# Cross attention: one copy for inputs and context, one for queries and keys, and the biases as one-row products on TensorE

## The reference

```
q = (query @ Wq.T + bq)   k = (key @ Wk.T + bk)   v = (value @ Wv.T + bv)     # query: layernorm(x); key, value: the context
scores = einsum('bhtd,bhsd->bhts', q, k) * D ** -0.5 + attn_mask              # D = 8
scores = where(pad, -inf, scores) + spatial_bias + directional_bias           # both are the same tensor (32, 16, 128, 128)
x = x + (softmax(scores) @ v) @ Wo.T + bo
```

## Time and profile before

| | |
|---|---|
| time, three runs | 644.36, 644.40, 647.64 us; median 644.4 |
| profiled execution | 645.74 us, span of its records 644.0 us |
| mean granted TensorE clock | 0.938 of full speed |
| busy over the span | PE 530.0, PEld 412.1, DVE 492.7, ACT 431.3, POOL 384.1 us |

### The profile page before, as it was taken

The page is one execution under the profiler, slowest core; times in us unless marked ns, Lnnn a source line. Parts: engine busy times, 40 slices in busy tenths (PEclk is TensorE's granted clock), DMA queues, the critical chain, the costliest instruction groups (busy, mean ns, idle before and its releaser), DMA issues.

```text
span 644.0 us, 16022 instructions
## 1 busy us (share of the span) xinstructions
PE 530.0 (82%) x4272; PEld 412.1 (64%) x4272; DVE 492.7 (77%) x1988; ACT 431.3 (67%) x1553; POOL 384.1 (60%) x430
## 2 busy tenths in 40 slices
PE   3589999999998967787777778777767699999986
PEld 2367877877877845555555555555545588788864
DVE  0446768777776646899999999999986788888872
ACT  3655687677776336899999999999995133333321
POOL 5124585564667467688888888888860444444430
PEclk9778999999999776998999998999996599999999
DMA  5930000000000334677777778888810000000000
GB/s 131 210 61 1 2 1 1 0 0 0 0 2 1 70 70 83 117 140 145 143 140 138 139 145 150 144 146 148 146 19 1 0 18 16 18 16 16 18 18 16
DMA packets 87512, 42.38 MB, mean 66 GB/s; under 512 B 7467, under 2 KB 87221, under 8 KB 87477
## 3 DMA queue, kind: packets, MB, share of 16 engines
q1 hardware_dynamic: 87476, 41.97, 34.7%
HBM read 39.86 MB, written 2.10 MB: 65 GB/s over the span
## 4 chain that ended last, share of the span: by engine, by line
PE 37%; DVE 17%; issue 8%; ACT 4%; DVEq 1%; POOL 1%; ACTq 0%; POOLq 0%
PE banks L1246 10%; DVE c_P L1037 8%; PE banks L932 5%; PE banks L1270 5%; PE banks L888 3%; ACT c_P L976 2%; PE banks L943 2%; DVE shared L1066 1%; DVE c_min L1037 1%; PE banks L468 1%; ACT shared L1303 1%; PE banks L919 1%; PE banks L898 1%; PE banks L1233 1%; PE banks L1240 1%
## 5 line engine op out<-in xcount | busy, mean ns | idle before, releaser
L976 ACT ACTIVATE c_P<-c_P,c_min 128x128 f32<-128x128 f32 x512 | 201.3, 425 | 0.0
L873 POOL TENSOR_TENSOR c_bias<-c_fside,c_cm 128x2048 f32<-128x2048 f32 x32 | 145.5, 4546 | 3.4 <-DVE c_cm L867 3.4
L1037 DVE CUSTOM_DVE_ANT_0 c_P<-banks,c_bias 128x128 f32<-128x128 f32 x512 | 117.1, 286 | 12.6 <-PE banks L888 7.4
L976 ACT ACTIVATION_READ_ACCUMULATOR c_P<-c_P,c_min 128x1 f32 x512 | 114.8, 224 | 0.0
L932 PE MATMUL banks<-ident,c_P 128*128 128x128 f32 x512 | 83.6, 294 | 5.5 <-ACT c_P L976 3.5
L932 PEld LDWEIGHTS banks<-ident,c_P 128*128 128x128 f32 x512 | 61.2, 150 | 18.7 <-ACT c_P L976 11.1
L1066 DVE COPY shared<-banks 128x512 f32<-128x512 f32 x96 | 65.9, 687 | 6.0 <-PE banks L932 6.0
L1481 POOL TENSOR_TENSOR xs<-shared,xs 128x512 fp32r<-128x512 f32 x8 | 10.8, 1352 | 87.0 <-ACT xs L1313 87.0
L1246 PE MATMUL banks<-um,lb_s 128*128 128x512 f32 x192 | 56.1, 407 | 2.7 <-ACT shared L1303 1.9
L919 PE MATMUL banks<-x_wT,shared 128*128 128x128 f32 x64 | 15.5, 326 | 40.2 <-DVE shared L1061 40.2
L1303 ACT ACTIVATE shared<-banks,bi_col 128x512 f32<-128x512 f32 x32 | 22.0, 688 | 39.2 <-PE banks L1246 39.2
(11 more groups left out here) (196 smaller groups left out, 1407.9 us busy)
## 6 DMA issues: line engine op xcount, KB each, us to landing
c_fside<-in_fside_Bx16xSxS_dram SPq DMA_DIRECT2D x64, 512.0 KB, 7.2
X<-in_x_dram SPq DMA_DIRECT2D x4, 512.0 KB, 5.0
c_ctx<-in_ctx_dram SPq DMA_DIRECT2D x32, 64.0 KB, 5.2
out_dram<-shared SPq DMA_DIRECT2D x8, 256.0 KB, 2.3
kmask_sb<-in_mask_BxS_bf_dram SPq DMA_DIRECT2D x1, 512.0 KB, 7.2
c_P<-in_L_ffn_wi_dram SPq DMA_DIRECT2D x1, 256.0 KB
c_P<-in_L_ffn_wo_dram SPq DMA_DIRECT2D x1, 256.0 KB
c_P<-in_L_ffn_lora_B_dram SPq DMA_DIRECT2D x4, 64.0 KB
```

The lines of the kernel that those rows point to most:

```text
L873: nc.gpsimd.tensor_tensor(fm[:, q, :, :], fs[:, q, :, :], bc(cm[:], XH), ALU.add).then_inc(C["fm"], 1)
L976: last = nc.scalar.activation(P[:, par, h, :], P[:, par, h, :], ACT.Exp, bias=mn[:, par, h:h + 1], scale=-1.0, accum_out=rsx[:, par, h:h + 1])
L1037: last = nc.vector.tensor_tensor_reduce(out=P[:, o, h, :], in0=score_bank(n + 1, i)[:, 128 * j:128 * j + 128], in1=fm[:, o, h, :], scale=- ...
```

## The change

The normalised input and the context are copied out of bank 0 by one instruction of 256 columns into a common tile, and so are queries and keys, by a plain copy. Their biases are put into the bank by TensorE: ahead of each projection a product of the bias row (one partition, 128 columns) with a row of ones. The scale of the queries moves into the weights and the bias row at setup. The block-diagonal keys are built from the new tile, which is double, so the wait of ScalarE for GpSimd loosens by one batch.

```diff
-        bq_raw = sb("bq_raw", [128, 1])
-        bq_col = sb("bq_col", [128, 1])
-        bk_col = sb("bk_col", [128, 1])
+        bias_rows = sb("bias_rows", [1, 3, 128])
+        bq_row, bk_row, bo_row = (bias_rows[:, i, :] for i in range(3))
...
-            for dst, src in ((bq_raw, x_bq), (bk_col, x_bk), (bv_col, x_bv)):
-                sp.dma_start(dst[:], src[:, None]).then_inc(s_xw, 16)
-            sp.dma_start(bo_row[:], x_bo[None, :]).then_inc(s_xw, 16)
+            for dst, src in ((bq_row, x_bq), (bk_row, x_bk), (bo_row, x_bo)):
+                sp.dma_start(dst, src[None, :]).then_inc(s_xw, 16)
+            sp.dma_start(bv_col[:], x_bv[:, None]).then_inc(s_xw, 16)
...
-            nc.scalar.copy(x_wT[:].rearrange("p i d -> p (i d)"), bank(6)).then_inc(s_wcopy, 1)
+            nc.scalar.activation(x_wT[:, 0, :], bank(6)[:, 0:128], ACT.Copy, scale=0.5 * float(XD) ** -0.5)
+            nc.scalar.copy(x_wT[:, 1:4, :].rearrange("p i d -> p (i d)"), bank(6)[:, 128:512]).then_inc(s_wcopy, 1)
...
-            nc.vector.tensor_scalar(bq_col[:], bq_raw[:], 0.5 * float(XD) ** -0.5, None, ALU.mult)
+            nc.vector.tensor_scalar(bq_row, bq_row, 0.5 * float(XD) ** -0.5, None, ALU.mult)
...
             def queries_keys():
                 need(pe, C["T"], n + 3)
-                nc.tensor.matmul(bank(0)[:, 0:128], x_wT[:, 0, :], xT2[:], start=True, stop=True)
-                nc.tensor.matmul(bank(0)[:, 128:256], x_wT[:, 1, :], cT[:, q, :], start=True, stop=True).then_inc(C["qkp"], 1)
+                for w, row in ((0, bq_row), (1, bk_row)):
+                    place = bank(0)[:, 128 * w:128 * w + 128]
+                    nc.tensor.matmul(place, row, ones[0:1, :], start=True, stop=False)
+                    last = nc.tensor.matmul(place, x_wT[:, w, :], xcT[:, q, w, :], start=False, stop=True)
+                last.then_inc(C["qkp"], 1)
...
-                nc.scalar.copy(xT2[:], bank(0)[:, 0:128])
-                nc.scalar.copy(cT[:, q, :], bank(0)[:, 128:256]).then_inc(C["T"], 1)
+                nc.scalar.copy(xcT[:, q, :, :].rearrange("p w t -> p (w t)"), bank(0)[:, 0:256]).then_inc(C["T"], 1)
...
-                nc.scalar.activation(qx[:, q, :], bank(0)[:, 0:128], ACT.Identity, bias=bq_col[:],
-                                     scale=0.5 * float(XD) ** -0.5).then_inc(C["q"], 1)
-                need(act, C["kbd"], n + 2)
-                nc.scalar.activation(kx[:], bank(0)[:, 128:256], ACT.Identity, bias=bk_col[:]).then_inc(C["k"], 1)
+                need(act, C["kbd"], n + 1)
+                nc.scalar.copy(qk[:, q, :, :].rearrange("p w t -> p (w t)"), bank(0)[:, 0:256]).then_inc(C["qk"], 1)
...
-                need(pool, C["k"], n + 3)
+                need(pool, C["qk"], n + 3)
                 need(pool, C["sc"], 4 * n + 4)
-                nc.gpsimd.tensor_tensor(kbd[:, q, :, :], bc(kx[:], XG), inner(k_mask[:], 128), ALU.mult).then_inc(C["kbd"], 1)
+                nc.gpsimd.tensor_tensor(kbd[:, q, :, :], bc(qk[:, q, 1, :], XG), inner(k_mask[:], 128), ALU.mult).then_inc(C["kbd"], 1)
```

More of the change, by code:

```diff
@@ L91, in decoder @@
         x_wT = sb("x_wT", [128, 4, 128])
-        bq_raw = sb("bq_raw", [128, 1])
-        bq_col = sb("bq_col", [128, 1])
-        bk_col = sb("bk_col", [128, 1])
+        bias_rows = sb("bias_rows", [1, 3, 128])
+        bq_row, bk_row, bo_row = (bias_rows[:, i, :] for i in range(3))
         bv_col = sb("bv_col", [128, 1])
         bv_wide = sb("bv_wide", [128, 128])
-        bo_row = sb("bo_row", [1, 128])
         x_bias = sb("x_bias", [128, 128])
@@ L132, in decoder @@
         lb_s = sb("lb_s", [128, 2, F], fp32r)
-        SHARED = 20736
+        SHARED = 18432
         shared = sb("shared", [128, SHARED])
@@ L279, in setup_tensor_2 @@
             nc.tensor.matmul(bank(6)[:, 0:128], bv_wide[:], x_wT[:, 3, :], start=True, stop=False)
-            nc.tensor.matmul(bank(6)[:, 0:128], ones[0:1, :], bo_row[:], start=False, stop=True)
+            nc.tensor.matmul(bank(6)[:, 0:128], ones[0:1, :], bo_row, start=False, stop=True)
             for c in range(FC):
@@ L827, in decoder @@
         xn2 = sb("c_xn", [128, 128])
-        cT = sb("c_cT", [128, 2, 128])
-        qx = sb("c_q", [128, 2, 128])
-        kx = sb("c_k", [128, 128])
+        xcT = sb("c_xcT", [128, 2, 2, 128])
+        qk = sb("c_qk", [128, 2, 2, 128])
         VPAD = XG * (32 + XD)
@@ L839, in decoder @@
         PTs = carve([128, 2, NI, 512])
-        xT2 = carve([128, 128])
         rx = carve([128, XH, XD])
@@ L845, in decoder @@
         C = {n: sem("c_" + n) for n in (
-            "stats", "aggr", "vareps", "rstd", "xn", "xbias", "Tp", "T", "qkp", "q", "k", "kbd", "cm", "fm",
+            "stats", "aggr", "vareps", "rstd", "xn", "xbias", "Tp", "T", "qkp", "qk", "kbd", "cm", "fm",
             "sc", "tt", "ex", "rc", "rx", "Rp", "RT", "pt", "ptD", "ptA", "pv", "oT", "yv", "v", "x2")}
@@ L879, in all_scores @@
             def all_scores():
-                need(pe, C["q"], n + 2)
+                need(pe, C["qk"], n + 2)
                 need(pe, C["kbd"], n + 2)
@@ L887, in all_scores @@
                     rows = slice(32 * i, 32 * i + 32)
-                    nc.tensor.matmul(score_bank(n + 1, i), qx[rows, o, :], kbd[rows, o, :, :].rearrange("p j s -> p (j s)"),
+                    nc.tensor.matmul(score_bank(n + 1, i), qk[rows, o, 0, :], kbd[rows, o, :, :].rearrange("p j s -> p (j s)"),
                                      start=True, stop=True).then_inc(C["sc"], 1)
@@ L907, in queries_keys @@
                 need(pe, C["T"], n + 3)
-                nc.tensor.matmul(bank(0)[:, 0:128], x_wT[:, 0, :], xT2[:], start=True, stop=True)
-                nc.tensor.matmul(bank(0)[:, 128:256], x_wT[:, 1, :], cT[:, q, :], start=True, stop=True).then_inc(C["qkp"], 1)
+                for w, row in ((0, bq_row), (1, bk_row)):
[3 more added lines that the diff above has]
+                last.then_inc(C["qkp"], 1)
             def outputs_values():
                 if project:
-                    need(pe, C["k"], n + 3)
+                    need(pe, C["qk"], n + 3)
                 else:
@@ L920, in outputs_values @@
                 if scores:
-                    last = nc.tensor.matmul(bank(0)[:, 128:256], cT[:, o, :], x_wT[:, 2, :], start=True, stop=True)
+                    last = nc.tensor.matmul(bank(0)[:, 128:256], xcT[:, o, 1, :], x_wT[:, 2, :], start=True, stop=True)
                 last.then_inc(C["yv"], 1)
```

## The result

The changed kernel takes 668.65 us, the median of four executions (662.75 to 669.18), where the kernel before takes 644.76 us beside it (644.36 to 647.64). The estimated ratio is 1.032, with a 95% interval of 1.028 to 1.037 (the two medians alone give 1.037). It is slower, as forecast, but by 24 us where 7.8 were forecast, and 12.7 us beyond the end of the range. The profiled execution has a span of 667.5 us against 644.0. Three of the four executions lie at 668.1 to 669.2 us with a mean granted clock of 0.922, the profiled one among them; the fourth took 662.75 us at 0.934.

The account below looks back on a forecast made before the run. VectorE was taken as the bound, with ScalarE a near miss. Steady stage 3.8, transition 3.8 and setup 0.2 made + 7.8 us on the median 644.4: 652.2 us, range 644.5 to 656 us.

Parts of the forecast that it names:

- near miss: Steady stage: ScalarE, though 100% busy, needs 7.62 us a batch against VectorE's 7.675, so it is not the bound.
- second rival: Steady stage: ScalarE is the bound after all, 7.6 us come off, 638 us in all; chance 0.13.
- The two instructions that ScalarE saves: Cross attention: merged copies and plain copies without bias save ScalarE 0.27 us a batch.
- the ring: Steady stage: ScalarE and TensorE wait on each other in a loop of 7.88 us, exceeding VectorE's 7.675; chance 0.48.
- 0.16 us a switch: TensorE's projections: cost of each change between one row and 128 at 2.4 GHz; four, with passes, make 1.08 us a batch.
- first rival: Added one-row products cost their passes alone, 0.44 us, within the margin of 0.59; 646.3 us in all; chance 0.27.
- the middle: Steady-stage loss over 28 batches: 3.8 us taken, between 5.2 and 2.4 if TensorE's weights start a little sooner.
- third rival: Steady stage: loop of ScalarE and TensorE dearer, 660 us at 0.22 us a switch, 669 at 0.29; low clock likewise; chance 0.12.
- Sum 3.8 us: Transition between the stages: total delay from four places on the chain of waits, at 216, 227, 243 and 255 us.
- First (216 us, full clock): + 1.08: Transition: L426 queued behind the projections at full clock, + 1.08 - 0.04 = + 1.0 us.
- third and fourth place: Transition at 243 and 255 us: products cost 1.3 us at a mixed clock, less 0.27, + 1.0 us each.
- + 0.2 us: Setup: one more weight-copy instruction and VectorE's scaling of 128 columns of one partition, half of both counted.

Follow-up runs that it names:

- full_rows: Changed kernel with bias products padded to 128 rows (bias in the first, zeros below) times a tile of ones: 648.5 us, ratio 1.003.
- rows_in_border: Changed kernel with one-row bias products only in the four steps at the border of the stages, 128-row ones elsewhere: 653.2 us, ratio 1.008.
- full_rows_long: Changed kernel with 128-row bias products, each followed by two more 128-row products of zeros: 665.0 us, ratio 1.029.
- no_bias: Changed kernel with both bias products, and so the biases, left out: 652.9 us, ratio 1.006.
- rows_in_steady: Changed kernel with 128-row bias products in the four steps at the border of the stages, one-row ones from step 2 on: 662.4 us, ratio 1.021.
- full_rows_values_on_scalar: Changed kernel with 128-row bias products and the copy of the values moved from VectorE to ScalarE: 646.0 us, ratio 0.998.

## Why the prediction was wrong

**The bound: right.** VectorE sets the steady stage. With the products left out its period stays 7.51 / 7.85 us and the time isn't 637 us; with full rows it stays too. ScalarE's 100% was a near miss. The second rival is refuted.

**The two instructions that ScalarE saves: right.** Worth nothing while the ring is open, 0.2 us a batch when it is closed.

**The cost of the products: right in kind, too small in size.** "0.16 us a switch" measured 0.19 to 0.20 at 2.4 GHz; at the low level four products take 2.9 us where a projection's two passes alone would take 0.43 each (1.72), so 0.30 us a switch where 0.29 was used. Four switches and four passes are 1.22 us, not 1.08. The first rival, passes alone, is what full_rows measured with 128 rows. The Trainium skill, page "TensorE: Matmul & The Clock Gate", section "Step-by-step: what each phase is for", has the weights' load depend on columns and not on rows. By that rule the one-row products would be as cheap as the full ones; the trace disagrees, 0.42 us a product against 0.22. The loads themselves do take the same time with one row as with 128 (two last 0.29 and 0.30 us in the batch at 404 us); the step between them is what costs.

**The ring: right in kind, too small in size, and then lowered once more.** Predicted 7.88 us: 0.27 + 5.11 + 2.39 + 0.11. Measured: 0.27 + 5.1 + 2.48 (404.46 to 406.94) + 0.16 (to 407.10) = 8.01, and L983 comes after 8.02. Against 7.675 that is 0.34 us a batch, where 0.2 stood. From the 0.2 the forecast worked out 5.2 us, and took 3.8, "the middle" between that and 2.4, for a gain that the rows didn't show. Measured: 7.2 us over 25 batches against the profile before, whose own 25 took 1.3 us more than those of full_rows (it has stretches like 300 to 310 us, at a clock of 0.83); against full_rows 8.5. The third rival has 669 us for a switch of 0.29 us. That this is nearly the measured time is chance: it needs a ring of 8.4 us, which is 8.01, and has nothing of the transition's loss. VectorE's alternation was not lost: its statistics (L1042) start at 387.40, 395.19, 403.42 and 411.21, 7.8 and 8.2 us apart.

**The transition: this is the step that failed.** "Sum 3.8 us" stood for it; the stretch grew by 14.5 us. Its places were right: L425 is queued behind the projections, and L989's wait is on the path. Its price was not. "First (216 us, full clock): + 1.08" took the clock of the kernel before for granted. In the profiled execution of the kernel after the clock is low at each of the four places, and every quartet takes 2.9 us, where the forecast had 1.5 (0.44 + 1.08) at the first. That is 4 x 2.93 = 11.7 us, less the projections alone in the chain before, 0.71, 0.73, 0.87 and 0.86: 8.5 us, where the forecast added 4.8 (1.08 twice, 1.3 twice) and took some off for ScalarE. Even by the kernel before 1.3 was too little at the third and fourth place: the two passes of L909 at the fourth take 0.43 us, the price of the low level, for which the forecast itself had 2.0. The rest, some 6 us, holds other products on the chain that now run at half speed, like L425 (2.01 us, was 1.09), and the fifth quartet (1.67 us at full clock). How it divides was not measured. The third rival names the clock, but as a delay that falls into no margin, and not as something that the change itself lowers. The experiments show that the time goes with the one-row products (6.5 to 9 us in profiles of like setup), and the profiles have more low clock with them (44 us in rows_in_border, against 27 in full_rows and 22 in full_rows_long). Whether these products lower the clock by themselves, and why it comes back sooner with full rows, stays open: no_bias has a mean clock as low in 7 of its 10 executions without them, and rows_in_steady was at the low level for 39 us before its first one.

**Setup and the rest.** "+ 0.2 us" for setup: the first 205 us were 2.1 us shorter. Between 40 and 50 us the clock was 1.00 where it was 0.59 before; over the experiments it lies between 0.60 and 1.00 there and doesn't go with the one-row products (1.00 in no_bias, 0.61 in rows_in_border). The last stage took 138.1 us against 135.5; no_bias has 137.9, rows_in_border 135.4. So neither belongs to the products, and their cause was not found. Nor is the early gain free of the transition: all five profiles with a clock of 1.00 at 40 to 50 us reach L434 1.7 to 4.4 us sooner than the others, and stay at the low level for 10 us or more around 210 to 220, where the others stay 7.

## What to carry to other kernels

A bias put in by TensorE was nearly free here (ratio 1.003) only when its product had as many rows as its neighbours: pad it with zero rows, or at least gather the small products so that the row count changes seldom. Before moving work to an engine "with slack", follow the ring through it: slack of 1.4 us a batch at one wait was worth only 0.59 us at another. And where a path runs through TensorE at a changing clock, price each added product at both levels for itself and for all that stands behind it. And look at the clock of every execution before reading one profile as the kernel's.

## What the runs showed of the hardware

- A step between a product of one row and one of 128 rows (f32) costs 0.19 to 0.20 us at 2.4 GHz and about 0.30 at 1.2 GHz, whichever way it goes: 1.66 us for four products with four steps, 1.28 with two, 0.90 with none. It neither halves nor stays with the clock.
- In the kernel after TensorE stays at 1.2 GHz from 229 to 270 us, though it is up to 97% busy (9.72 of 10 us at 260 to 270). With 128 rows in place of one, the windows from 230 to 270 have clocks of 0.66 to 0.83 in full_rows, 0.70 to 1.00 in full_rows_long and 0.50 to 1.00 in full_rows_values_on_scalar.
- The same instructions can take 4.5 us longer in one execution than in another over some 60 us (64.2 us in rows_in_steady, 59.7 in full_rows, up to the fifth quartet).
- One and the same program has times some 5 us apart, which go with its mean granted clock (645 us at 0.943, 650 at 0.93). A difference under 1% between two medians of this kernel can be no more than how often each came.
